# A Mamba-like mixer whose second chunk is reached by an across-chunks product instead of a chunk state, with one sequence's output products moved into the drain

## What is computed

```python
h = tok_ref(x)            # embedding, attention: softmax over queries, (softmax(q k)) v
h = h + attn_ref(layernorm(h))   # the mixer (below), itself ending in "+ x"
h = h + ffn_ref(layernorm(h))    # 8 experts, top 2 per token, capacity 1024 rows each
```

```python
Y_diag = jnp.einsum('bcln,bcsn,bhcls,bcshp->bclhp', Cc, Bc, Lm, Xc)
decay_states = jnp.exp(a_cs[..., -1:] - a_cs)
states = jnp.einsum('bcln,bhcl,bclhp->bchpn', Bc, decay_states, Xc)
...
Y_off = jnp.einsum('bcln,bchpn,bhcl->bclhp', Cc, prev_states, jnp.exp(a_cs))
return (Y_diag + Y_off).reshape(b, l, h, p)
```

## Time and profile before

| | |
|---|---|
| median of 3 runs | 926.17 us |
| the profiled execution: time, span | 926.9 us, 925.2 us |
| TensorE busy (products), share of the span | 904.3 us, 98% |
| VectorE, ScalarE, GpSimd busy | 633.4, 528.6, 503.8 us |
| mean granted TensorE clock | 0.996 |
| experts start | 548.54 us |

### The profile page before, as it was taken

The page is one execution under the profiler, slowest core; times in us unless marked ns, Lnnn a source line. Parts: engine busy times, 40 slices in busy tenths (PEclk is TensorE's granted clock), DMA queues, the critical chain, the costliest instruction groups (busy, mean ns, idle before and its releaser), DMA issues. The chain is left out here.

```text
span 925.2 us, 17776 instructions
## 1 busy us (share of the span) xinstructions
PE 904.3 (98%) x5832; PEld 806.5 (87%) x5832; DVE 633.4 (68%) x1698; ACT 528.6 (57%) x1097; POOL 503.8 (54%) x498
## 2 busy tenths in 40 slices
PE   8999999999999999999999979999999999999998
PEld 7888798888888888888888779999999999999997
DVE  1587889888988898889889644646464646464633
ACT  1767776677667766776667434444443434343533
POOL 5656877887778777876775522223232323232343
PEclk9999999999999999999999989999999999999999
DMA  7940011001000000000000044343434342523221
GB/s 211 321 154 17 30 47 34 23 34 34 13 23 14 24 13 23 14 25 12 12 14 5 25 138 122 70 109 74 108 70 112 67 115 63 119 58 79 23 58 46
DMA packets 49398, 59.13 MB, mean 64 GB/s; under 512 B 6304, under 2 KB 44683, under 8 KB 49360
## 3 DMA queue, kind: packets, MB, share of 16 engines
q1 hardware_dynamic: 35920, 42.14, 14.1%
q0 software_dynamic: 13440, 16.50, 10.7%
HBM read 33.62 MB, written 30.67 MB: 69 GB/s over the span
## 5 line engine op out<-in xcount | busy, mean ns | idle before, releaser
L690 POOL DMA_INDIRECT out<-ye,tok_slot x56 | 96.0, 1713 | 250.0 <-DMA out<-ye,tok_slot 128.0
L973 ACT ACTIVATE hf<-bank 128x512 f32<-128x512 f32 x128 | 79.3, 620 | 187.1 <-PE bank L1814 187.0
L1423 DVE TENSOR_TENSOR h_lo<-hf,h_hi 128x512 fp32r<-128x512 f32 x128 | 88.8, 694 | 101.5 <-ACT h_hi L975 100.1
L1812 PE MATMUL bank<-w_hi,h_hi 128*128 128x256 f32 x512 | 146.1, 285 | 0.0
L1813 PE MATMUL bank<-w_lo,h_hi 128*128 128x256 f32 x512 | 144.9, 283 | 0.0
L1814 PE MATMUL bank<-w_hi,h_lo 128*128 128x256 f32 x512 | 144.9, 283 | 0.0
L1122 DVE SCALAR_TENSOR_TENSOR xc<-bank,cw,xc 128x253 f32<-128x253 f32 (+2 forms) x288 | 128.2, 469 | 1.9 <-ACT xc L799 0.4
L1812 PE MATMUL bank<-xe_hi,w_hi 128*128 128x512 f32 x256 | 100.0, 391 | 0.0
L1813 PE MATMUL bank<-xe_lo,w_hi 128*128 128x512 f32 x256 | 99.8, 390 | 0.0
L1814 PE MATMUL bank<-xe_hi,w_lo 128*128 128x512 f32 x256 | 99.7, 389 | 0.0
L1813 PEld LDWEIGHTS bank<-w_lo,h_hi 128*128 128x128 f32 x512 | 98.3, 192 | 0.0
(11 more groups left out here) (223 smaller groups left out, 2352.3 us busy)
## 6 DMA issues: line engine op xcount, KB each, us to landing
w_raw<-w SPq DMA_DIRECT2D x16, 1024.0 KB
slots_dram<-zero_row SPq DMA_DIRECT2D x1, 8320.0 KB, 29.9
xe<-slots_dram SPq DMA_DIRECT2D x15, 520.0 KB, 4.5
out<-hb SPq DMA_DIRECT2D x16, 256.0 KB, 2.1
w_raw<-in_wT SPq DMA_DIRECT2D x2, 644.0 KB, 6.2
out<-zero_row SPq DMA_DIRECT2D x1, 1024.0 KB, 32.1
slots_dram<-rows,slot POOLq DMA_INDIRECT x64
out<-ye,tok_slot POOLq DMA_INDIRECT x64
```

Of the source, the lines that this page charges most:

```text
L690: g.indirect_dma_start(out, bass.IndirectOffsetOnAxis(ap=tok_slot[q][:, j:j + 1], axis=0), ye[q][:, j, :], None, compute_op=ALU.add).then_ ...
L973: sc.activation(hf[m % 2][:, :], h_bank[i % H_BANKS][:, :], ACT.Gelu_apprx_tanh)\
L1423: vc.tensor_tensor(h_lo[:, m, :], hf[m % 2][:, :], h_hi[:, m, :].bitcast(F32), ALU.subtract)\
L1812: te.matmul(out_, hi, rhi, start=first_, stop=False)
```

## The change

1. The chunk state goes. `state_inputs` now makes, in place of the transpose of B of chunk 0, the product of B of chunk 0 and C of chunk 1 (`across`, copied by ScalarE where `bs` was). `across_chunks` takes the place of `chunk_state`: `across` times `xdec`, straight into bank 3, which `carried_y` reads. `from_state` (TensorE) and `state` (ScalarE) are gone.
2. On VectorE `carried_y` stands ahead of `first_y`: the transposes of the first gated chunk go into bank 3 too.
3. The output products of the second to last sequence leave the last full half and stand in the drain: chunk 0 behind `state_inputs`, chunk 1 behind the second `x_to_rows`, where 11 of the 15 fillers of the drain were. Its `gated_root` on GpSimd moves too, behind `decayed_x` of the drain.
4. In the drain, GpSimd waits for the second `decay_scores` before it scales xs; ScalarE copies `across` ahead of the third silu and copies x to rows later; VectorE reads both chunks of x from PSUM.
5. In the last half `describe_rows` is done by VectorE, between `router_top` and `slots_of`, no longer by GpSimd.
6. Three fillers in place of six ahead of the experts.

The diff, cut to what the text speaks of:

```diff
@@ -386,7 +384,7 @@
         FILL = dict(t=4, scores=4, attend=5, hT=18, dt=8)
-        DRAIN = dict(rows=2, seg0=1, seg2=8, state=2, out=2)
+        DRAIN = dict(state=2, out=2)
         LAST = dict(v2T=10, route=2, choices=9)
@@ -636,6 +634,8 @@
                         decayed_x(b, q)
+                        gated_root(t, p)
+                        pool.wait_ge(m_ready[KD - 1][q], m_ready[KD - 1].now(b, q))
                         skip_x(b, q, 0)
@@ -644,7 +644,7 @@
                         second_root(b, q)
-                    describe_rows(t, p)
+                        describe_rows(t, p)
                     scatter_rows(t, p)
@@ -664,7 +664,6 @@
                     segment_inputs(f, p, 0)
-                    gated_root(b, q)
                     free_rows(t, p)
@@ -821,7 +820,7 @@
                 act.wait_ge(btg_psum[p], btg_psum.now(r, p))
-                sc.activation(bs[p][:, :], bank[p][3][:, 0:NS], ACT.Copy)
+                sc.activation(across[p][:, :], bank[p][3][:, 0:P], ACT.Copy)
                 copy(ea[p][:, :], bank[p][3][:, 3 * P:3 * P + NH], bs_ready[p], ACT.Exp)
@@ -834,17 +833,13 @@

-            def late_rows(r, p):
-                act.wait_ge(xdt_ready[p], xdt_ready.now(r, p))
-                copy(xs[p][:, 1, :], bank[1 - p][2][:, :], xs_ready[p])
+            def late_rows(r, p, c):
+                act.wait_ge(xdt_ready[p], xdt_ready.now(r, p, c + 1))
+                copy(xs[p][:, c, :], bank[(p, 1 - p)[c]][2][:, :], xs_ready[p])

             def x_rows(r, p, c):
                 act.wait_ge(xs_psum[p], xs_psum.now(r, p, c + 1))
                 copy(xs[p][:, c, :], bank[p][XS_BANK[c]][:, :], xs_ready[p])
-
-            def state(r, p):
-                act.wait_ge(state_psum[p], state_psum.now(r, p))
-                copy(st[p][:, :], bank[p][3][:, :], st_ready[p])

@@ -878,17 +873,16 @@
                     silu_z(b, q, 1)
+                    state_copy(b, q)
                     silu_conv(b, q, 2)
-                    state_copy(b, q)
-                    x_rows(b, q, 0)
                     decay(b, q, 0)
                     decay(b, q, 1)
                     end_decay(b, q)
+                    late_rows(b, q, 0)
                     carry_exp(b, q)
                     decay(b, q, 2)
                     decay(b, q, 3)
-                    late_rows(b, q)
-                    state(b, q)
+                    late_rows(b, q, 1)
                     square(b, q, 0)
@@ -931,8 +925,6 @@
                     normed(f, p)
-                if b:
-                    state(b, q)
                 if f:
@@ -1147,10 +1139,10 @@

-                def times_dt_early(r, p):
-                    dve.wait_ge(xs_psum[p], xs_psum.now(r, p))
-                    vc.tensor_tensor(heads(xdt[p][:, 1, :]), heads(bank[1 - p][2][:, :]),
-                                     bc(dt_[p][:, 1, :].unsqueeze(2), [P, NH, HD]), ALU.mult).then_inc(xdt_ready[p], 1)
+                def times_dt_early(r, p, c):
+                    dve.wait_ge(xs_psum[p], xs_psum.now(r, p, c + 1))
+                    vc.tensor_tensor(heads(xdt[p][:, c, :]), heads(bank[(p, 1 - p)[c]][2][:, :]),
+                                     bc(dt_[p][:, c, :].unsqueeze(2), [P, NH, HD]), ALU.mult).then_inc(xdt_ready[p], 1)

@@ -1180,7 +1172,7 @@
                     dve.wait_ge(yo_psum[p], yo_psum.now(r, p))
-                    carried_y.last = back.mark(vc.tensor_tensor(heads(y[p][:, 1, :]), heads(bank[p][2][:, :]),
+                    carried_y.last = back.mark(vc.tensor_tensor(heads(y[p][:, 1, :]), heads(bank[p][3][:, :]),
                                                                 bc(ea[p][:, :].unsqueeze(2), [P, NH, HD]), ALU.mult))
@@ -1270,6 +1262,15 @@

+                def describe_rows(t, p):
+
+                    dve.wait_ge(tok_next[1 - p], tok_next.now(t, 1 - p))
+                    dve.wait_ge(ohs_ready[p], ohs_ready.now(t, p))
+                    vc.tensor_copy(rows[p][:, :, C_TOK].bitcast(I32), tok_iota[:, :])
+                    vc.tensor_copy(rows[p][:, :, C_E0], topf[p][:, :, 0])
+                    vc.tensor_tensor(rows[p][:, :, C_W0:C_W0 + 2], top[p][:, :, 0:2],
+                                     bc(linv[p][:, :].unsqueeze(2), [P, KD, 2]), ALU.mult).then_inc(row_info[p], 1)
+
                 def with_bias(r, p):
@@ -1285,14 +1286,14 @@
                     segment_inputs(b, q, seg_hi, a_hi)
-                    times_dt(b, q, 0)
+                    times_dt_early(b, q, 0)
                     segment_inputs(b, q, seg_lo, a_lo)
-                    times_dt_early(b, q)
+                    times_dt_early(b, q, 1)
                     decay_scores(b, q, 0)
                     decay_scores(b, q, 1)
                     residual_sum(t, p, p)
+                    carried_y(b, q)
                     first_y(b, q)
-                    carried_y(b, q)
                     second_y(b, q)
@@ -1329,14 +1330,16 @@
                 if b:
+                    carried_y(b, q)
                     first_y(b, q)
-                    carried_y(b, q)
                 if f:
                     split_hT(f, p)
                 if b:
                     second_y(b, q)
                 if f:
                     dt_in(f, p)
+                if not f:
+                    describe_rows(t, p)
                 if t:
@@ -1590,7 +1593,7 @@
                     pe.wait_ge(a_ready[p], a_ready.now(r, p))
-                    te.transpose(bank[where][3][:, 0:P], xc[p][:, KI, 0:P], ident[:, :])
+                    te.matmul(bank[where][3][:, 0:P], xc[p][:, KI, 0:P], xc[p][:, KI + 1, P:2 * P], start=True, stop=True)
                     for c in range(KD):
@@ -1625,13 +1628,13 @@

-                def chunk_state(r, p):
+                def across_chunks(r, p):

                     pe.wait_ge(decay_ready[p], decay_ready.now(r, p, 2))
                     pe.wait_ge(bs_ready[p], bs_ready.now(r, p))
                     pe.wait_ge(xdec_ready[p], xdec_ready.now(r, p))
-                    te.matmul(bank[p][3][:, :], bs[p][:, :], xdec[p][:, :], start=True, stop=True)\
-                        .then_inc(state_psum[p], 1)
+                    te.matmul(bank[p][3][:, :], across[p][:, :], xdec[p][:, :], start=True, stop=True)\
+                        .then_inc(yo_psum[p], 1)

@@ -1644,12 +1647,6 @@

-                def from_state(r, p):
-                    pe.wait_ge(st_ready[p], st_ready.now(r, p))
-                    pe.wait_ge(decay_ready[p], decay_ready.now(r, p))
-                    te.matmul(bank[p][2][:, :], xc[p][:, KI + 1, P:2 * P], st[p][:, :], start=True, stop=True)\
-                        .then_inc(yo_psum[p], 1)
-
                 def to_yT(r, p, c):
@@ -1701,19 +1698,17 @@
                     project_z(b, q, 1)
                     state_inputs(b, q, p)
-                    keep_clock(p, DRAIN["rows"])
+                    project_rows(t, p, 0, p)
                     x_to_rows(b, q, 0)
-                    x_to_rows(b, q, 1, p)
-                    keep_clock(p, DRAIN["seg0"])
                     segment_sums(b, q, 0)
                     segment_sums(b, q, 1)
-                    keep_clock(p, DRAIN["seg2"])
+                    x_to_rows(b, q, 1, p)
+                    project_rows(t, p, 1, p)
                     segment_sums(b, q, 2)
                     segment_sums(b, q, 3)
                     keep_clock(p, DRAIN["state"])
-                    chunk_state(b, q)
+                    across_chunks(b, q)
                     own_chunk(b, q, 0)
-                    from_state(b, q)
                     own_chunk(b, q, 1)
                     to_yT(b, q, 0)
@@ -1794,7 +1787,7 @@
                     project_channels(f, p, 2)
-                if b:
+                if b and nf:
                     project_out(b, q)
@@ -1862,7 +1855,7 @@
                         ins.then_inc(signal_, 1)
-                    keep_clock(0, 6)
+                    keep_clock(0, 3)
                     return
```

More of the change, by code:

```diff
@@ L237, in lm_block @@
         gm = pair("gm", [P, KD, P])
-        bs = pair("bs", [P, NS])
+        across = pair("across", [P, P])
         xdec = pair("xdec", [P, DI])
-        st = pair("st", [P, DI])
         h2 = pair("h2", [P, KD, DM])
@@ L327, in lm_block @@
         m_ready = [signal(f"m{c}_ready") for c in range(KD)]; skip_ready = signal("skip_ready", 2)
-        state_psum = signal("state_psum"); st_ready = signal("st_ready")
         yd_psum = signal("yd_psum", 2); yo_psum = signal("yo_psum")
@@ L814, in state_copy @@
                 act.wait_ge(btg_psum[p], btg_psum.now(r, p))
-                sc.activation(bs[p][:, :], bank[1 - p][3][:, 0:NS], ACT.Copy)
+                sc.activation(across[p][:, :], bank[1 - p][3][:, 0:P], ACT.Copy)
                 copy(ea[p][:, :], bank[1 - p][3][:, 3 * P:3 * P + NH], bs_ready[p])
```

## The result

| | before | after |
|---|---|---|
| median | 926.29 us (925.28 to 926.82, 4 runs) | 941.38 us (936.16 to 953.92, 4 runs) |
| ratio | | 1.0138, 95% interval 1.0077 to 1.0199 |
| profiled execution: time, span | 926.9, 925.2 us | 945.77, 944.0 us |
| mean granted TensorE clock | 0.996 | 0.974 |

The change makes the kernel slower by 1.4% (by 1.6% between the medians); the forecast was 926.5 us. The 18.8 us between the two spans lie here: the cut at the first full half comes 1.24 us sooner (63.66 for 64.90), thirteen halves take 20.94 us more, from there to the experts it is 0.95 us less (79.12 for 80.07), and the experts take 376.7 us in both.

What follows compares the result with a forecast made beforehand. TensorE was taken to bound the kernel, VectorE a close second. Terms +2.5 - 0.75 + 0.1 - 0.65 - 0.63 - 0.3 = +0.3 us gave 927.2 us profiled, 926.5 us median; range 922.5 to 930.0 us.

Steps and rivals of the forecast that it cites:

- the term of the thirteen halves: Thirteen full halves: each takes 31.24 us, 406.1 against 403.6 in all, +2.5 us.
- rival 5: Halves: the clock falls in each as TensorE idles, 14 times at least 1 us; 940 us or more; chance 0.05.
- The wait at y: Thirteen halves: TensorE waits about 1.4 us at the transposes of y for VectorE's gate.
- Two kinds of halves: Thirteen halves: short and long kinds become equal, 31.2 us each, with no wait for the normed rows.
- Rival 1: Thirteen halves: the long half stays, +5.3 us in place of +2.5, so 929.3 us; chance 0.22.
- First half with a mixer: First half with a mixer: y has slack, so the half gains 0.86 - 0.11 us; -0.75 us.
- Drain: Drain: products with the decays no longer alternate with GpSimd's scaling, so y comes sooner; -0.65 us, between -0.1 and -1.1.
- the row I went by: Drain: GpSimd's root does not hold VectorE's product up; by the skill's lock rule the term would be -0.1 us.
- VectorE sets the pace of the drain: Drain: VectorE's gapless work keeps the 3.3 us of moved output products from being a full gain.
- Last rows: Last half: describing the rows leaves GpSimd from between two scatters; -0.63 us, or -1.13 if the issue gap also shrinks.
- Fillers ahead of the experts: Ahead of the experts: six passes move the start 0.8 us forward, partly at lower clock; -0.3 us, between +0.6 and -0.8.
- Drain and tail together: Behind the thirteen halves: last full half +0.1, drain -0.65, last rows -0.63, fillers ahead of the experts -0.3 us.

Runs made afterwards that it cites:

- e1: The changed kernel with six identity products nobody reads, in TensorE's wait ahead of the transposes of y's first chunk; 928.02 us.
- e3: The changed kernel with chunk state and old order back in all halves, so only the drain and tail edits differ from the kernel before; 925.79 us.
- e5: The changed kernel with three identity products nobody reads in TensorE's wait at the transposes of y, filling about half of it; 925.85 us.
- e8: The changed kernel with dt products ahead of the transposes of y's first chunk and 20 identity products in place of 38 behind the last half; 923.76 us.
- e7: The changed kernel with the four small dt products moved ahead of the transposes of y's first chunk; 923.99 us.
- e2: The kernel before with only the edits of the halves: state product gone, carried part first; no drain or tail edits; 946.21 us.
- e9: The changed kernel with dt products ahead of the transposes of y, plus one identity product ahead of dt; 925.88 us.
- e10: As e9, with 20 identity products in place of 38 behind the last half; 926.67 us.

## Why the prediction was wrong

**The step that failed** is the term of the thirteen halves. +2.5 us was forecast and +20.9 measured, of which about 18.7 are falls of the clock, a cost that the sum put at nothing: it stood in rival 5 alone, with a chance of 0.05. The reason for that chance was one row: the only fall in the trace before, its last microsecond aside, came in an idle time of 4.7 us, "much longer" than 1.4. One fall says that so long an idle time is enough; it says nothing on a shorter one. The trace before does hold waits of 0.5 us in its halves and of 0.78 in its drain without a fall, and from there to 4.7 us it is silent. My forecast had the new wait in all thirteen halves and yet counted each at its own length and full clock. That rival 5's time came out right (14 times at least 1 us, 940 or more; measured 941.4) is luck: the profile has seven falls in the thirteen halves and not fourteen, at 3.1 or 1.6 us each and not 1, and the same kernel ran in 936 us and in 954.

**The wait at y**: right in place and cause, 1.25 us for 1.4. Halves of 31.13 us for 31.24, so thirteen cost +1.1 for +2.5; e1, with the wait filled, has +1.6.

**Two kinds of halves**: right that the long kind goes. In e1 all thirteen last 31.09 to 31.26 us. Rival 1 did not happen.

**First half with a mixer**: -0.68 for -0.75 (30.41 us, from 33.25 to 63.66, for 31.09). The other 0.56 of the 1.24 us by which the first full half comes sooner are there before this half begins. The half ahead of it takes 22.11 us in both, so they lie in the start, which the change leaves alone: in the profiles with this start the first half begins anywhere from 10.8 to 11.7 us.

**Drain**: the products with the decays came down as forecast. This is e3's timeline of VectorE and TensorE:

```profile
508.44 1.47 DVE L1165 TENSOR_TENSOR seg<-seg,gm 128x1024 f32<-128x1024 f32 x1
...
510.11 1.23 DVE L1165 TENSOR_TENSOR seg<-seg,gm 128x1024 f32<-128x1024 f32 x1 [0.20 <-ACT seg L739]
...
512.30 1.08 PE L1662 MATMUL bank<-st,xc 128*128 128x512 f32 x2
...
513.36 0.69 DVE L1172 TENSOR_TENSOR y<-y,sz 128x512 f32<-128x512 f32 x1
...
514.94 0.61 PE L1507 MATMUL bank<-ident,y 128*128 128x128 f32 x4
```

Both products are done by 511.34, 42.39 us after the last cut, where it was 43.53 before. In e3 y is gated at 514.05 and taken at 514.94: with the state product TensorE is the later one, and only 0.10 us is won. Without it, in e5, y is taken 45.40 us after the cut for 46.09: -0.69, forecast -0.65. The Trainium skill (SBUF — State Buffer, section SBUF: two separate sides) has the two engines lock each other out for a whole instruction, where VectorE's has two inputs in SBUF, as here. In e3 GpSimd's root runs from 508.79 beside the first of these products and takes 1.71 us, where one beside other work took 0.73, while VectorE's product takes 1.47 for 1.25. The two overlap and both are slowed: neither the full lock of the rule nor the free passage of the row I went by. The next product waits for ScalarE, so it costs little here. The 3.3 us of output products taken off TensorE ahead of all this became 2.3 us of waiting at the z products (0.69 and 1.59 in e3): that VectorE sets the pace of the drain was right.

**Last rows**: the last scatter stands 9.05 us after the first for 10.23, and no gap above the usual 0.30 is left between two scatters (changed kernel):

```profile
552.47 0.97 POOL L623 DMA_INDIRECT slots_dram<-rows,slot  x1 [0.30 <-issue]
553.75 0.97 POOL L623 DMA_INDIRECT slots_dram<-rows,slot  x1 [0.30 <-issue]
```

That is -1.18, the bound of -1.13 and not the -0.63 I took: the 0.82 of issue went with the description.

**Fillers ahead of the experts**: -0.3 was forecast. With a smooth block (e5) the time from the last scatter to the experts falls from 9.69 to 8.74 us, -0.95; with a halting one it grows, to 11.01 in e1. But e5's experts begin 2.3 us before the clock returns, and then take 377.61 us for 376.66 before:

```profile
547.14:549.44 2.30, 2.30 (x6) 1.82 (x7) 1.95 (x7) 0.00 (x0) 0.00 (x0) 0.50 0.56 193
```

Counted from the last cut, the experts' start moves forward by 2.8 us and the clock's return by 0.7 only, and the experts' +0.95 is as much as this term had won: about 0 for -0.3. Drain and tail together give -2.76 up to the experts in e5, -1.8 with the experts' own +0.95, for -1.48 forecast; and -0.95 in the changed kernel, whose block halts and where one more short fall, at 511.8 us, lies in the last full half.

So at full clock the forecast was about right: with three fillers in the wait the changed kernel takes 925.85 us, within 0.2% of before, with +1.7 in the thirteen halves for +2.5 and -1.8 behind them for -1.5. The clock turned no change into 1.4%.

The best version is e8: the whole change, dt ahead of the transposes of y, and 20 fillers behind the last half, 923.76 us, faster than before by 0.26% (0.16 to 0.35%) and than the changed kernel by 17.6 us in the median. It can't be told from e7, with 38 fillers.

## What to carry to other kernels

Where TensorE is busy throughout, work taken off it ahead of a late operand becomes idle time, and that idle time can cost more than its length: look for what the granted clock does behind it, and if the trace before has no wait of that size, among products as small, give the fall a real chance. Such a hole is to be filled, best with products whose operands are already there; here 0.8 us of small products turned +15 us into -2. Look also at what a gain runs into next: in e3, 38 halting fillers hid all that the drain and the tail had won, and in e5 experts that began sooner began at the lower clock.

## What the runs showed of the hardware

- A single wait of 1.23 to 1.29 us in a half of 31 us, TensorE busy otherwise, was met by a fall of the granted clock to the lower level for 3.4 or 6.8 us, at a cost of 1.6 or 3.1 us. It happened at 7 of 11 such waits of one execution (the changed kernel) and at 4 of 9 in another (e2); five falls in a row stood 34.1 us apart. Waits of 0.5 us in each of thirteen halves (e5) brought none.
- A longer wait, of 1.57 to 1.66 us, among products of 512 columns brought no fall in any of eleven profiles.
- The clock also fell with no wait shown in the 28 us ahead of it, behind products of 8 and 64 columns (e9 at 209.1 us, e10 at 210.7 and 398.4).
- A row of identity products that ran through at 0.115 us a pass in some kernels halted after its 39th or 40th pass in others, in steps of about 0.72 us, with nothing in the profile to wait for.
